# Storing and reloading the relative scores of a decoder layer's cross attention in two halves of 64 rows

## The reference, cut to what matters

```python
QEr  = jnp.einsum('bhsd,ld->bhsl', q, Er)        # relative scores, 1024 x 1024 for each head
Srel = _skew(QEr)                                # row s is shifted to the left by 1023 - s
QK   = jnp.einsum('bhsd,bhtd->bhst', q, k)
attn = (QK + Srel) / math.sqrt(dh)
attn = jnp.where(causal, attn, -jnp.inf)         # column t counts only for t <= s
attn = jax.nn.softmax(attn, axis=-1)
```

## Time and profile before

| | |
|---|---|
| median of 3 runs | 4048.88 us (4045.84 to 4054.18) |
| the profiled execution: its time, its span | 4051.76 us, 4050.0 us |
| TensorE (PE) busy | 3819.8 us, 94% |
| VectorE, ScalarE, GpSimd busy | 61%, 39%, 22% |
| moved by DMA | 671.68 MB, mean 166 GB/s |

### The profile page before, as it was taken

The page is one execution under the profiler, slowest core; times in us unless marked ns, Lnnn a source line. Parts: engine busy times, 40 slices in busy tenths (PEclk is TensorE's granted clock), DMA queues, the critical chain, the costliest instruction groups (busy, mean ns, idle before and its releaser), DMA issues. The chain is left out here.

```text
span 4050.0 us, 91371 instructions
## 1 busy us (share of the span) xinstructions
PE 3819.8 (94%) x37104; PEld 2361.9 (58%) x37104; DVE 2471.8 (61%) x4870; ACT 1599.6 (39%) x3247; POOL 900.9 (22%) x1005
## 2 busy tenths in 40 slices
PE   5999999989999999899999989999999889999997
PEld 2677644656766446567765455676654565544445
DVE  3777635877776347777772477888834784222224
ACT  2444324754443147644441376444413772100002
POOL 2333200213333002133330021333300211322221
PEclk8999999999999999999999999999999999999998
DMA  8333439744334398543341985433328855666666
GB/s 261 103 93 94 143 126 332 265 151 114 98 93 125 118 327 266 179 119 98 98 119 72 337 270 190 127 99 93 102 79 332 272 195 186 170 149 153 153 148 187
DMA packets 317181, 671.68 MB, mean 166 GB/s; under 512 B 27840, under 2 KB 120752, under 8 KB 313664
## 3 DMA queue, kind: packets, MB, share of 16 engines
q1 hardware_dynamic: 273792, 616.80, 47.8%
q0 software_dynamic: 15024, 34.41, 4.6%
q10 hardware_dynamic: 27968, 14.82, 1.6%
HBM read 383.40 MB, written 210.04 MB: 147 GB/s over the span
## 5 line engine op out<-in xcount | busy, mean ns | idle before, releaser
L751 ACT ACTIVATE sc<-sc,nmax 128x1024 f32<-128x1024 f32 x512 | 587.0, 1147 | 773.2 <-DVE nmax L990 772.8
L698 POOL TENSOR_SCALAR sc<-sc,pinv 128x1024 f32<-128x1024 f32 x512 | 574.4, 1122 | 1171.6 <-DVE pinv L998 1159.8
L990 DVE CUSTOM_DVE_ANT_0 sc<-psum,w_and_tables 128x1024 f32<-128x1024 f32 x512 | 603.7, 1214 | 98.0 <-PE psum L1305 84.1
L1363 PE MATMUL psum<-pts,wct 32*64 32x256 f32 x8192 | 459.8, 376 | 8.1 <-PEq L1358 4.5
L1363 PE MATMUL psum<-xall,wct 32*64 32x256 f32 x8192 | 460.0, 376 | 7.3 <-issue 7.2
L1348 PE MATMUL psum<-xt,w_and_tables 128*128 128x256 f32 x1792 | 415.4, 385 | 25.1 <-PEq L1345 25.1
L1150 DVE CUSTOM_DVE_ANT_0 sc<-psum,big 128x896 f32<-128x896 f32 (+7 forms) x512 | 364.2, 754 | 102.0 <-PE psum L1574 87.8
L1348 PEld LDWEIGHTS psum<-xt,w_and_tables 128*128 128x128 f32 x1792 | 332.5, 190 | 129.8 <-issue 68.5
L751 ACT ACTIVATE sc<-sc,xmax 128x896 f32<-128x896 f32 (+7 forms) x512 | 394.9, 773 | 11.7 <-DVE xmax L1150 11.6
L1015 DVE STREAM_TRANSPOSE pts<-sc 128x1024 f32<-128x1024 f32 (+3 forms) x340 | 331.2, 974 | 111.1 <-PE psum L1363 68.1
L1363 PEld LDWEIGHTS psum<-pts,wct 32*64 32x64 f32 x8192 | 309.6, 132 | 98.5 <-issue 53.4
(11 more groups left out here) (225 smaller groups left out, 5180.3 us busy)
## 6 DMA issues: line engine op xcount, KB each, us to landing
wct<-xall SPq DMA_DIRECT2D x576, 128.0 KB, 2.4
big<-skew_d SPq DMA_DIRECT2D x48, 1024.0 KB, 5.8
big<-skew_d SPq DMA_DIRECT2D x48, 768.0 KB, 4.5
w_and_tables<-rows_d SPq DMA_DIRECT2D x64, 448.0 KB, 5.0
big<-skew_d SPq DMA_DIRECT2D x32, 896.0 KB, 4.8
w_and_tables<-w_dram SPq DMA_DIRECT2D x26, 1024.0 KB, 5.8
big<-skew_d SPq DMA_DIRECT2D x32, 640.0 KB, 7.7
w_and_tables<-wqkv_dram SPq DMA_DIRECT2D x32, 512.0 KB, 3.6
```

The lines of the kernel that those rows point to most:

```text
L698: pool.tensor_scalar(sc[k % 4][:, :], sc[k % 4][:, :], pinv[:, k % 4:k % 4 + 1], 1.0, ALU.mult, ALU.mult).then_inc(probs_scaled, 1)
L751: act.activation(tile, tile, ACT.Exp, bias=least, scale=-1.0, accum_out=total).then_inc(probs_ready, 1)
L990: dve.tensor_tensor_reduce(sc[k % 4][:, :], SLOT[h], table[h][:, off:off + S], -1.0, BIG, ALU.add, ALU.min, nmax[:, k % 4:k % 4 + 1]).then ...
L1363: mm = pe.matmul(OSUM[HEAD[h], a, :], v_all[rows, ST * (b % GROUPS) + b // GROUPS, HEAD[h]], ptf[h][rows, QG * b:QG * b + QG], start=(b == ...
```

## The change

A tile of 128 rows is stored with two transfers, and a unit is loaded with two transfers, one for each half of 64 rows. For rows 0 to 63 the first 64 stored columns are left out (the shifted read of those rows starts 64 columns or more to the right), and so these rows are loaded without their last 64 columns, which lie above the diagonal and are masked. Each half has its own place in `skew_d`. The semaphores count 32 for each tile or unit where they counted 16.

```diff
+BAND = P // 2
+BANDS = [(0, P - BAND), (BAND, 0)]
+STORED = 16 * len(BANDS)
...
+        def band_starts(w):
+
+            sizes = [HPQ * BAND * (w - skip) for _, skip in BANDS]
+            return [sum(sizes[:g]) for g in range(len(BANDS))]
...
-                    sp.wait_ge(rel_stored[made % 3], 16 * (made // 3 + 1))
-                    at = skew_d[v, P * w * heads[0] + P - 1:P * w * heads[0] + P]
-                    src = bass.AP(tensor=at.tensor, offset=at.offset, ap=[[w - 1, P], [P * w, nh], [1, w]])
-                    sp.dma_start(skw[u % 4].rearrange("p (h n) -> p h n", h=nh)[:, :, 0:w], src
-                                 ).then_inc(skew_loaded[u % 4], 16)
+                    sp.wait_ge(rel_stored[made % 3], STORED * (made // 3 + 1))
+                    for (row, skip), start in zip(BANDS, band_starts(w)):
+                        m = w - skip
+                        first = start + BAND * m * heads[0] + BAND - 1
+                        at = skew_d[v, first:first + 1]
+                        src = bass.AP(tensor=at.tensor, offset=at.offset, ap=[[m - 1, BAND], [BAND * m, nh], [1, m]])
+                        sp.dma_start(skw[u % 4].rearrange("p (h n) -> p h n", h=nh)[row:row + BAND, :, 0:m], src
+                                     ).then_inc(skew_loaded[u % 4], 16)
...
-                    sp.dma_start(skew_d[v - v % ST + t, 0:HPQ * P * w].rearrange("(h p n) -> p h n", h=HPQ, p=P),
-                                 relb[v % 3][:, :, 0:w]).then_inc(rel_stored[v % 3], 16)
+                    for (row, skip), start in zip(BANDS, band_starts(w)):
+                        m = w - skip
+                        sp.dma_start(skew_d[v - v % ST + t, start:start + HPQ * BAND * m]
+                                     .rearrange("(h p n) -> p h n", h=HPQ, p=BAND),
+                                     relb[v % 3][row:row + BAND, :, skip:w]).then_inc(rel_stored[v % 3], 16)
...
-                    pool.wait_ge(skew_loaded[u % 4], 16 * (u // 4 + 1))
+                    pool.wait_ge(skew_loaded[u % 4], STORED * (u // 4 + 1))
...
-                        act.wait_ge(rel_stored[v % 3], 16 * (v // 3))
+                        act.wait_ge(rel_stored[v % 3], STORED * (v // 3))
...
-                        dve.wait_ge(rel_stored[v % 3], 16 * (v // 3))
+                        dve.wait_ge(rel_stored[v % 3], STORED * (v // 3))
```

More of the change, by code:

```diff
@@ L626, in batch @@
                         load_skewed(1)
-                sp.wait_ge(rel_stored[2], 16 * len(range(2, XV, 3)))
+                sp.wait_ge(rel_stored[2], STORED * len(range(2, XV, 3)))
                 def load_swapped(qd):
@@ L637, in batch @@
                     if u == 4:
-                        sp.wait_ge(rel_stored[1], 16 * len(range(1, XV, 3)))
+                        sp.wait_ge(rel_stored[1], STORED * len(range(1, XV, 3)))
                         load_swapped(0)
@@ L669, in batch @@
                 for i in range(3):
-                    sp.sem_inc(rel_stored[i], -16 * len(range(i, XV, 3)))
+                    sp.sem_inc(rel_stored[i], -STORED * len(range(i, XV, 3)))
                 def store_rows(dst):
@@ L737, in batch @@
                 for i in range(4):
-                    pool.sem_inc(skew_loaded[i], -16 * (NU // 4))
+                    pool.sem_inc(skew_loaded[i], -STORED * (NU // 4))
             with pool.Fori(0, B - 1):
@@ L904, in xexp @@
                     exp_tile(k, scx[u % 2][:, span(u, i)], xmax[:, k:k + 1], xsum[:, k:k + 1])
-                act.wait_ge(rel_stored[0], 16 * len(range(0, XV, 3)))
+                act.wait_ge(rel_stored[0], STORED * len(range(0, XV, 3)))
                 for u in range(NU + 4):
@@ L1177, in scale_output @@
                                       ).then_inc(ot_scaled, 1)
-                dve.wait_ge(rel_stored[0], 16 * len(range(0, XV, 3)))
+                dve.wait_ge(rel_stored[0], STORED * len(range(0, XV, 3)))
                 def row_stats(t):
```

## The result

| | before | after |
|---|---|---|
| median | 4049.34 us (4 runs, 4045.84 to 4054.18) | 4248.89 us (4 runs, 4240.63 to 4251.12) |
| the profiled execution's span | 4050.0 us | 4246.1 us |
| moved by DMA | 671.68 MB | 654.95 MB |
| TensorE busy | 3819.8 us | 3885.4 us |

The ratio is 1.0486, with a 95% interval of 1.0473 to 1.0498; by the medians it is 199.5 us slower, or 50 us in each of the four batches, though 16.7 MB less is moved. The prediction had said slower, at 4345 us; its range (4095 to 4440) holds the result, but the loss is two thirds of the 296 us forecast.

The account below looks back on a forecast made before the run. In cross attention, TensorE and the DMA engines were both taken as near their limit in stage one. + 57 us there and + 17 in stage two made 74 a batch, 296 in four: about 4345 us, range 4095 to 4440.

Parts of the forecast that it names:

- The mechanism: Cross attention: transfers of 64 neighbouring rows make 16 DMA engines hinder each other, so packets take longer; forecast at 225 GB/s, chance 0.68.
- the swapped copies: Groups of four 64-row transfers inside SBUF in the old trace, 238 to 242 GB/s; used to price half transfers at 225.
- stage two: Cross attention's second part, 684 to 850 us in the first batch: forecast 17 us longer, two of its four parts covered.
- stage one: Cross attention's relative scores, 569 to 684 us in the first batch: forecast 172 us instead of 115, + 57 us.
- upper bound of 217 GB/s for a half: From the Trainium skill: 64 partitions in a row reach 8 of 16 ports, giving at most some 217 of 435 GB/s.
- At 225 GB/s that takes 163 us: In stage one, 36.7 MB still to move at the rate of partial partitions, before the borders are added.
- The rival with less contention: Engines split between the halves: at 270 GB/s + 27 us in stage one, + 2 in stage two; 4140 us, chance 0.18.
- 3 us at three borders: In stage one, DMA engines run dry between quads, about 3 us each time, adding 9 us.
- The wait named as next: In stage two, what is late next is GpSimd's mask, then VectorE's addition; no separate size given.
- TensorE's clock: May fall from 2.4 to 1.2 GHz while TensorE waits for buffers; left out of the sum, put into the upper end.
- Full rate: Rival: half transfers run at 374 GB/s and above, so fewer bytes save 11 us; 4038 us, chance 0.08.
- the issue alone: Rival: full rate, but 31 waits for stores each end up to 0.36 us later, 11 us; 4060 us, chance 0.06.

## Why the prediction was right in kind and its loss half too large

- **The mechanism** (packets get longer where 16 engines reach for half of the partitions) holds: in the store of three blocks, packets of 4096 B took 165 ns in the mean from 568.5 to 570.5 us (the middle) and 282 ns from 572.5 to 574.5 (the ends). Of three kernels with two transfers and all columns, the one that splits heads has + 0.1%, even and odd rows + 0.3%, two blocks of neighbouring rows + 5.8%. That the swapped copies, which are SBUF to SBUF, gave the price for transfers to and from HBM, holds in stage two and not in stage one; nor does the prediction's upper bound of 217 GB/s for a half: the stores move 233 with one half in flight and 368 with both.
- **"At 225 GB/s that takes 163 us"**, in the sum of stage one, is the step that failed. 36.8 MB (252 GB/s x 146 us) moved in 0.89 x 146 = 130 us of full DMA time, or 283 GB/s: the rate starts at 200 and climbs to 368. That is 33 us a batch less than forecast. The rival with less contention had this price: "if half of the engines get ahead of the others" at 270 GB/s, + 27 us in stage one. It got a chance of 0.18 because the swapped copies alternate between the halves too and show no climb; but they last for some 3 us and a quad for 36, so the price was applied far beyond the length in which it had been seen.
- **"3 us at three borders"** was too little: 146 - 130 = 16 us without full DMA time in place of the 9 of the sum. The kernel before had 11.5 of them (0.10 x 115), which the sum left out. 163 + 9 = 172 was to be 130 + 16 = 146: **+ 31 instead of + 57 us**.
- **Stage two** was right: 224 / 1.04 = 215 GB/s and **+ 20 us in the first batch, + 17 over all four, for + 17**. Its parts were not: two of them were to be covered (0.68 and 0.75 busy before), and now none of the four windows is below 0.96; the queue is behind when it comes to them. The wait named as next, VectorE for GpSimd's mask, is there with 85.8 us for 4.2.
- **TensorE's clock** was left out of the sum and fell. In the second quad it stands at 0.50 or 0.51 from 627 to 639 us, the lower level of 1.2 GHz, after TensorE had waited for buffers in the two windows ahead (busy for 2.21 and 1.00 of 3 us). Over stage one the mean of 0.89 means some 32 of 146 us at that level (0.11 x 146 / 0.5). From 633 to 639 TensorE is busy all the time at the low clock while the DMA share falls to 0.92 and 0.84, so there it may well be what holds the stores back. The second and the third quad, each from its first store to the next quad's, bound this roughly:

```profile
605.65:643.36 37.71, 33.47 (x141) 11.72 (x139) 12.62 (x13) 10.60 (x13) 0.64 (x1) 0.82 0.90 255
643.36:679.78 36.42, 30.15 (x182) 15.78 (x180) 12.76 (x14) 10.60 (x13) 0.64 (x1) 0.95 0.86 245
```

The second quad has some 10 us more at the low clock (0.82 for 0.95) and takes 1.3 us longer. At that price 32 us make some 4 of the 31 us, an estimate from one pair of quads; no run took the clock away.

- **The rivals.** Full rate falls by the stores and the loads in halves alone, each of them slower; the issue alone falls by the split over heads, and its longer form by the even and odd rows. Less contention was right for stage one, by the mechanism it named (one group of engines on each half, as the packets show), and wrong for stage two.

**What stays open.** Why the loads of stage two stay slow though both halves are in flight together there. The trace doesn't say which engine moves a packet, so it doesn't tell whether the engines that hinder each other are on the same half in the loads and on different halves in the stores. Nor was it shown what sets the engines apart in the stores.

## What to carry to other kernels

Bytes left out of a transfer can be lost again by the rows that the transfer is left with: here 5.6% less of these bytes was worth 33 us, and the two blocks of 64 neighbouring rows that it took cost 233. Before such a change is made, the same number of transfers with the same rows, split over another dimension (heads, or every second row), shows whether the count or the rows matter. A price that is read from a short burst is good for the length of that burst; in a longer stretch the rate has to be looked at over time.

## What was not expected of the hardware

- The rate of half stores climbs from 200 to 368 GB/s within some 18 us at an unchanged share near 1, as packets of both halves come to be in flight together, and falls back when the queue has run dry. Half loads stay at 204 to 240 GB/s in the four windows of stage two with both halves in flight.
- It matters which rows a transfer has, not only how many: 373 GB/s for rows 32 to 95, 221 for 0 to 31 and 96 to 127, in one store.
- An issue took 0.36 us. For 64 rows it takes 0.57 at least, and up to 3.0 us for a load and 2.8 for a store where the engines are slow; the 17 units of the earlier trace rows are issued in 66.7 us instead of 61.25. The kernel with even and odd rows has issues of 0.6 us and loses only 0.3%, so an issue of that length is not the cause; what lengthens an issue further was not measured.
